# The base product of a feed-forward layer as three rounded products, and later places for GpSimd's weight splits, in an eight-layer fp32 kernel

## The reference

```python
def _L0_ffn_ref(x, W_base, b_base, W_router, A_stack, B_stack):
    logits = xf @ W_router.T
    probs = softmax(logits)
    topk_p, topk_i = top_k(probs, 2); topk_p = topk_p / sum(topk_p)
    combine = sum(one_hot(topk_i, 8) * topk_p[..., None])
    h = einsum('nd,erd->ner', xf, A_stack) * combine[..., None]
    lora_out = einsum('ner,eor->no', h, B_stack) * SCALING
    base_out = xf @ W_base.T + b_base
    return base_out + lora_out
...
# L1 xattn: 16 query heads in 4 groups, head size 96, keys and values from context and latents
# L1 ffn: the same form as L0 ffn.  L2 xattn: one head, Q = x Wq + bq, K = ctx Wk + bk, no values
```

## Time and profile before

| | |
|---|---|
| median of three runs | 1699.91 us |
| profiled execution, its own time | 1700.22 us |
| its span in the trace | 1698.1 us |
| TensorE busy | 1617.2 us, 95% |
| VectorE busy | 931.6 us, 55% |
| ScalarE busy | 743.7 us, 44% |
| GpSimd busy | 371.1 us, 22% |
| L0F from its first base product | 880.15 us |
| L1F from its first base product | 1295.96 us |

### The profile page before, as it was taken

One profiled execution on the slowest core, in us unless ns is written; L12 is line 12 of the kernel. 1 busy time (PEld: TensorE's weight loads), 2 busy tenths in 40 slices (PEclk: granted clock), 3 DMA queues, 4 the chain that ended last, 5 costly groups with the idle time before them and its releaser, 6 DMA issues.

```text
span 1698.1 us, 25834 instructions
## 1 busy us (share of the span) xinstructions
PE 1617.2 (95%) x9028; PEld 1288.3 (76%) x9028; DVE 931.6 (55%) x2467; ACT 743.7 (44%) x2174; POOL 371.1 (22%) x266
## 2 busy tenths in 40 slices
PE   9999999999999999999988999999999899899875
PEld 8888888888888888888764968787876687655454
DVE  5652534525345253452577766757485857455787
ACT  4542443424434244342423453636273231677742
POOL 3210212102121021110014100000002533355452
PEclk9999999999999999999999999999999999999989
DMA  5111101111011010110431000000004212000001
GB/s 183 54 41 49 41 28 52 40 43 47 28 52 41 31 58 28 49 40 27 138 121 65 14 8 6 0 12 0 1 26 158 79 50 90 14 14 14 1 1 49
DMA packets 34137, 76.09 MB, mean 45 GB/s; under 512 B 5536, under 2 KB 18336, under 8 KB 31904
## 3 DMA queue, kind: packets, MB, share of 16 engines
q1 hardware_dynamic: 34080, 75.36, 13.0%
HBM read 73.25 MB, written 2.10 MB: 44 GB/s over the span
## 4 chain that ended last, share of the span: by engine, by line
PE 72%; DVE 17%; ACT 5%; issue 3%; DVEq 2%; POOL 1%; DMA 0%; POOLq 0%; ACTq 0%; SPq 0%
PE banks L973 14%; PE banks L983 10%; PE banks L1070 10%; PE banks L1174 9%; PE banks L1278 5%; PE banks L1250 3%; PE banks L1041 3%; DVE sA L1647 3%; PE banks L1056 2%; ACT sA L673 2%; PE banks L1387 2%; PE banks L1401 2%; PE banks L1380 1%; PE banks L1048 1%; PE banks L1408 1%
## 5 line engine op out<-in xcount | busy, mean ns | idle before, releaser
L1670 DVE TENSOR_TENSOR x_res<-banks,x_res 128x512 f32<-128x512 f32 x120 | 82.9, 692 | 207.6 <-PE banks L1070 207.2
L973 PE MATMUL banks<-cT,w_k 128*128 128x512 f32 x720 | 179.8, 398 | 0.0
L983 PE MATMUL banks<-w_v,cT 128*128 128x512 f32 x768 | 179.8, 392 | 0.0
L973 PE MATMUL banks<-xT,w_q 128*128 128x512 f32 x720 | 175.4, 396 | 0.0
L673 ACT ACTIVATE sA<-sA,nmA 128x128 f32<-128x128 f32 x256 | 99.5, 392 | 166.5 <-DVE nmA L1647 165.5
L1070 PE MATMUL banks<-w_o,atT 128*128 128x512 f32 x720 | 170.3, 393 | 2.1 <-DVE x_res L1670 2.0
L983 PEld LDWEIGHTS banks<-w_v,cT 128*128 128x128 f32 x768 | 142.7, 188 | 28.9
L1070 PEld LDWEIGHTS banks<-w_o,atT 128*128 128x128 f32 x720 | 134.1, 188 | 31.3 <-DVE x_res L1670 2.4
L973 PEld LDWEIGHTS banks<-xT,w_q 128*128 128x128 f32 x720 | 131.9, 188 | 25.5
L973 PEld LDWEIGHTS banks<-cT,w_k 128*128 128x128 f32 x720 | 130.8, 188 | 25.2
L1654 DVE TENSOR_SCALAR rsA<-smA 128x4 f32<-128x4 f32 x64 | 15.7, 245 | 185.5 <-ACT sA L673 185.5
(11 more groups left out here) (243 smaller groups left out, 3257.7 us busy)
## 6 DMA issues: line engine op xcount, KB each, us to landing
w_raw_k<-in_w0k SPq DMA_DIRECT2D x16, 512.0 KB, 3.3
w_raw_v<-in_w0v SPq DMA_DIRECT2D x8, 1024.0 KB, 7.2
w_raw_q<-in_w0q SPq DMA_DIRECT2D x15, 512.0 KB, 3.2
w_raw_o<-in_w0o SPq DMA_DIRECT2D x15, 512.0 KB, 3.2
cTp<-in_ctxT SPq DMA_DIRECT2D x12, 512.0 KB, 4.0
wq_raw<-in_wq SPq DMA_DIRECT2D x1, 3072.0 KB, 11.5
wo<-in_wo SPq DMA_DIRECT2D x1, 3072.0 KB, 21.2
kT<-in_ctxT SPq DMA_DIRECT2D x4, 512.0 KB, 6.5
```

Of the source, the lines that this page charges most:

```text
L973: mm = pe.matmul(dst, w[l][:, c, h * P:(h + 1) * P], t[r][:, c, half * 512:(half + 1) * 512], start=n == 0, stop=n == 3 * DC - 1)
L983: mm = pe.matmul(dst, cT[l][:, c, b * P:(b + 1) * P], wv_[r][:, c, :], start=n == 0, stop=n == 3 * DC - 1)
L1670: dve.tensor_tensor(x_res[:, b, :], bank(6 + b % 2), x_res[:, b, :], ALU.add).then_inc(S("o_added"), 1)
```

## The change

L0F's base product takes the three-product form. Its weight gets a high part `f0p[0]` (ScalarE, in `last_pair` between the second probability store and the second attended store) and a low part `f0p[1]` (GpSimd, behind the split of w_q). TensorE waits for it (`wf_lo`) and, for each block, for xn's low part, which VectorE now makes in L0F too (`PARTS` has L0F). The raw weight and the parts get other places in SBUF, and wq1, wk1 and wv1 are now split in place (the low part is written over the raw weight). The splits of wq1, wq2 and wk2 on GpSimd are cut otherwise and wait for VectorE's xn; wq1's high part is made in four pieces, one for each group of query heads, and TensorE waits for the piece of a group ahead of its queries.

```diff
-PARTS = {L1X: 0, L1F: 1, L2X: 2, L2F: 3}
+PARTS = {L0F: 0, L1X: 1, L1F: 2, L2X: 3, L2F: 4}
...
@@ GpSimd
             split("o", NHP - 1)
             split("q", NHP - 1)
+            pool.wait_ge(S("wf_hi"), 1)
+            for c in range(DC):
+                e = pool.tensor_tensor(f0p[1][:, c, :], ffn["f0"]["base"][:, c, :], f0p[0][:, c, :].bitcast(F32), ALU.subtract)
+            e.then_inc(S("wf_lo"), 1)
...
+            def queries_rest(kv):
+                k = slice(NCH * P * kv, NCH * P * (kv + 1))
+                pool.wait_ge(S("wq1_hi"), kv + 1)
+                pool.tensor_tensor(wq1[1][:, :, k], wq1_raw[:, :, k], wq1[0][:, :, k].bitcast(F32), ALU.subtract)\
+                    .then_inc(S("wq1_lo"), 1)
+
+            def x1_first():
+                pool.wait_ge(S("xn_ready"), NB * (L0F - 1) + NB)
+                queries_rest(0)
+
             def x1_end():
+                pool.wait_ge(S("wkv1_lo"), 2)
+                queries_rest(1)
                 pool.wait_ge(S("ffn_out"), NB)
                 context_rest(0)
-                rest(wq1, wq1_raw, "wq1", 1, 3, DC)
-            pairs_split(pool, ffn_pool(L0F, tb["f0"]), nothing, lambda: rest(wq1, wq1_raw, "wq1", 1, 0, 3), x1_end)
+                queries_rest(2)
+                queries_rest(3)
+            pairs_split(pool, ffn_pool(L0F, tb["f0"]), nothing, x1_first, x1_end)
...
             def x2_end():
+                pool.wait_ge(S("xn_ready"), NB * (L1F - 1) + NB + 2)
+                rest(wk2, raw2["k"], "wk2")
                 context_rest(NPAIR)
-                rest(wk2, raw2["k"], "wk2", 1, 2, DC)

             def x2_weights():
+                pool.wait_ge(S("xn_ready"), NB * (L1F - 1) + NB)
                 rest(wq2, raw2["q"], "wq2")
-                rest(wk2, raw2["k"], "wk2", 1, 0, 2)
...
@@ ScalarE, last_pair
                 store_pT(p, 1)
+                act.wait_ge(S("ffn_ld"), 64)
+                act.activation(f0p[0][:], ffn["f0"]["base"][:], ACT.Copy).then_inc(S("wf_hi"), 1)
                 store_at(p, 1)
...
@@ TensorE, ffn_pe
-                        if second:
-                            wait_parts(L, i, j)
+                        wait_parts(L, i, j)
                         for c in range(DC):
-                            if second:
-                                for n, (l, r) in enumerate(PASSES):
-                                    pe.matmul(bank(4 + j), xnTp[l][:, c, t], f1p[r][:, c, :], start=c == 0 and n == 0, stop=False)
-                            else:
-                                pe.matmul(bank(4 + j), xnT[:, c, t], w["base"][:, c, :], start=c == 0, stop=False)
+                            for n, (l, r) in enumerate(PASSES):
+                                pe.matmul(bank(4 + j), xnTp[l][:, c, t], parts[r][:, c, :], start=c == 0 and n == 0, stop=False)
...
-                if second:
-                    pe.wait_ge(S("wf_lo"), 1)
+                pe.wait_ge(S("wf_lo"), second + 1)
...
@@ TensorE, x1_pe
                     if more:
+                        pe.wait_ge(S("wq1_lo"), kv + 2)
                         queries(kv + 1, 0, 2)
...
@@ VectorE, ahead of L0F's pairs
+            for j in range(2):
+                part_lo(L0F, 0, j)
             ffn_dve(L0F, 4, 2.0)
```

More of the change, by code:

```diff
@@ L133, in build @@
         rr = sb(ctx_a, "rr", [P, NB])
+        f0_high = sb(ctx_a, "f0base_0", [P, DC, D], F32R)
         xw = [xw_all[:, k] for k in range(4)]
@@ L141, in build @@
         ctx_g = ExitStack()
-        ffn["f0"] = dict(base=sb(ctx_g, "f0base", [P, DC, D]), ra=sb(ctx_g, "f0ra", [P, DC, NE + NE * RANK]),
-                         up=sb(ctx_g, "f0up", [P, D]))
+        sb(ctx_g, "f0_pad", [P, 2 * DC * PT2])
+        ffn["f0"] = dict(ra=sb(ctx_g, "f0ra", [P, DC, NE + NE * RANK]), up=sb(ctx_g, "f0up", [P, D]))
         ctx_g.close()
@@ L152, in build @@
         sb(ctx_f, "f0_rest", [P, 32])
+        ctx_g = ExitStack()
+        ffn["f0"]["base"] = sb(ctx_g, "f0base", [P, DC, D])
+        ctx_g.close()
+        ctx_g = ExitStack()
+        f0p = [f0_high, sb(ctx_g, "f0base_1", [P, DC, D], F32R)]
+        ctx_g.close()
         ctx_g = ExitStack()
@@ L210, in build @@
         ctx_x.close()
-        wq1 = [sb(ctx_1, f"wq1_{l}", [P, DC, H1 * HD1], F32R) for l in range(2)]
-        wk1 = [sb(ctx_1, f"wk1_{l}", [P, DC, KV1 * HD1], F32R) for l in range(2)]
-        wv1 = [sb(ctx_1, f"wv1_{l}", [P, DC, KV1 * HD1], F32R) for l in range(2)]
+        in_place, raw1 = {}, {}
+        for n, cols in (("wq1", H1 * HD1), ("wk1", KV1 * HD1), ("wv1", KV1 * HD1)):
+            high_1 = sb(ctx_1, n + "_0", [P, DC, cols], F32R)
+            ctx_x = ExitStack()
+            raw1[n] = sb(ctx_x, n + "_raw", [P, DC, cols])
+            ctx_x.close()
+            in_place[n] = [high_1, sb(ctx_1, n + "_1", [P, DC, cols], F32R)]
+        wq1, wk1, wv1 = (in_place[n] for n in ("wq1", "wk1", "wv1"))
+        wq1_raw, wk1_raw, wv1_raw = (raw1[n] for n in ("wq1", "wk1", "wv1"))
         wo1 = sb(ctx_1, "wo1", [P, NCH * KV1, D])
-        ctx_x = ExitStack()
-        wq1_raw = sb(ctx_x, "wq1_raw", [P, DC, H1 * HD1])
-        ctx_x.close()
         q1 = sb(ctx_1, "q1", [HD1, 2, G1, PT2], F32R)
@@ L534, in _ @@
             pairs_ahead(pool, x1_pool)
-            rest(f1p, ffn["f1"]["base"], "wf")
+            rest(f1p, ffn["f1"]["base"], "wf", 2)
             def x2_end():
+                pool.wait_ge(S("xn_ready"), NB * (L1F - 1) + NB + 2)
+                rest(wk2, raw2["k"], "wk2")
                 context_rest(NPAIR)
-                rest(wk2, raw2["k"], "wk2", 1, 2, DC)
             def x2_weights():
+                pool.wait_ge(S("xn_ready"), NB * (L1F - 1) + NB)
                 rest(wq2, raw2["q"], "wq2")
-                rest(wk2, raw2["k"], "wk2", 1, 0, 2)
             pairs_split(pool, ffn_pool(L1F, tb["f1"]), nothing, x2_weights, x2_end)
@@ L552, in x2_pool @@
                     context_rest(NPAIR + i + 2)
-            pairs_split(pool, x2_pool, lambda: rest(w2, zp2, "wf", 2), nothing, nothing)
+            pairs_split(pool, x2_pool, lambda: rest(w2, zp2, "wf", 3), nothing, nothing)
             rsqrt(NPAIR * (L2F - 1) + 1)
@@ L924, in _, with x1_queries, x1_first @@
             store_xnT(L0F, 0)
-            def x1_queries():
+            def x1_queries(kv):
+                k = slice(NCH * P * kv, NCH * P * (kv + 1))
+                act.activation(wq1[0][:, :, k], wq1_raw[:, :, k], ACT.Copy).then_inc(S("wq1_hi"), 1)
+            def x1_first():
                 act.wait_ge(S("wq1_ld"), 16)
-                high(wq1[0], wq1_raw[:], "wq1")
+                x1_queries(0)
+                x1_queries(1)
             def x1_keys_values():
@@ L932, in x1_keys_values, with x1_end @@
                 high(wv1[0], wv1_raw[:], "wkv1")
-            pairs_split(act, ffn_act(L0F), x1_queries, x1_keys_values, lambda: context_high(0))
+            def x1_end():
+                context_high(0)
+                x1_queries(2)
+                x1_queries(3)
+            pairs_split(act, ffn_act(L0F), x1_first, x1_keys_values, x1_end)
             pairs_ahead(act, x1_act)
@@ L1178, in ffn_pe @@
             def ffn_pe(L, f):
-                w, second = ffn[f], int(L == L1F)
+                w, second, parts = ffn[f], int(L == L1F), f1p if L == L1F else f0p
                 def body(i, last):
@@ L1550, in _ @@
             f3_turn(0)
-            pe.wait_ge(S("wf_lo"), 4)
+            pe.wait_ge(S("wf_lo"), 5)
             f3_gate_up(0)
```

8 lines of the change are left out of this document (2 added, 6 removed).

## The result

| | before | changed |
|---|---|---|
| median of the runs, us | 1700.01 (4 runs) | 1685.66 (4 runs, 1681.33 to 1687.29) |
| ratio | | 0.9913, 95% interval 0.9891 to 0.9934 |
| profiled execution, us | 1700.22 | 1684.36 |
| its span, us | 1698.1 | 1682.0 |
| mean granted clock over the span | 0.984 | 0.986 |

The change makes the kernel 0.9% faster. It is inside what case (a) allowed for itself (1685.5 to 1691.5), but only just.

What follows compares the result with a forecast made beforehand. TensorE bounds the kernel (72% of the chain), stalled in both third pairs by GpSimd's bulk splits holding up VectorE's tiny instructions. 8.7 + 6.7 - 4.2 = 11.2 us gained, giving 1688.7 us; range 1684 to 1693.5.

Steps and rivals of the forecast that it cites:

- case (a): Whole program: both stalls gone, 4 us lost in front, 4 at the two ends; 1688.7 us (1685.5 to 1691.5); chance 0.60.
- L0F, pairs 1 to 3: First feed-forward layer, first three token pairs: 32.8 us where 44.1 stood, 11.3 us won.
- L0F, fourth pair: First feed-forward layer, last pair to the first context product: 17.0 us against 14.37, 2.6 us lost.
- L1F, all: Second feed-forward layer: 8.2 us won in the third pair, 1.5 lost in the fourth, 6.7 us together.
- part 1: Both feed-forward layers: GpSimd's later splits end the third pairs' stalls, so each takes 10.93 us instead of 21.04 and 19.16.
- part 2: First layer's base product in three rounded products: 1.27 us a pair shorter, only 0.60 left because VectorE's cycle bounds it.
- rival (c): New waits at keys and context bring the lower clock and collisions: gain 5 to 8.5 us, 1691.5 to 1695; chance 0.18.
- part 3: Last head pair before the first feed-forward layer: f0base's split delays VectorE 2.9 us, with clock 4.2 lost (0.5 to 6).
- half low-clock stretch: Last head pair: idle growing from 0.9 to 3.9 us brings half a lower-clock stretch, 1.3 us lost.
- (b): Front costs 0.5 us, or periods are 10.17: gain 14.9, with both 17 us, 1683 to 1685.5; chance 0.17.
- (d): Stalls moved into the fourth pairs by splits running into their routing: 7.1 us lost, 1707 us; chance 0.03.
- (e): Whole program: no change that can be told, the gain given back at a transfer; chance 0.02.

Runs made afterwards that it cites:

- E6: The changed kernel run again without a further edit, on one chip with two variants: 1683.29 us, ratio 0.9926 to the kernel before.
- E1: The changed kernel without the rounded product and its f0base split, only the later splits of wq1, wq2 and wk2 kept: 1679.01 us, ratio 0.9899.
- E2: The changed kernel with the splits of wq1, wq2 and wk2 back in their old places, rounded product kept: 1697.29 us, ratio 1.0008.
- E5: The kernel before, with GpSimd's wq1 split in the first layer's third pair cut from three instructions into twelve: 1691.53 us, ratio 0.9978.
- E4: The changed kernel with f0base split earlier, ahead of the w_q split, beside the head pair before: 1683.24 us, ratio 0.9925.
- E8: The changed kernel with GpSimd's f0base split moved behind the last x times gate, second run of this kernel: 1682.05 us, ratio 0.9909.
- E9: The changed kernel with GpSimd's f0base split cut from four instructions into sixteen, same place and bytes: 1682.66 us, ratio 0.9891.
- E3: The changed kernel with GpSimd's f0base split moved behind the last x times gate, first run of this kernel: 1681.07 us, ratio 0.9908.
- E7: The re-timing alone run again, without the rounded product and its f0base split, on another chip: 1681.01 us, ratio 0.9912.

## Why the prediction was right, step by step

| step | forecast | first profile | E6 |
|---|---|---|---|
| L0F, pairs 1 to 3, us | 3 x 10.93 | 10.45, 10.90, 10.80 | 10.46, 10.90, 10.81 |
| L0F, fourth pair | 17.0 | 16.50 | 17.26 |
| L1F, all | 49.3 | 49.78 | 49.77 |
| last head pair of L0X, loss | 4.2 | 2.4 | 2.4 |
| rest of the program, gain | 0 | 2.4 | |

**The stalls (part 1).** Right, in cause and size. E1 has the gain without the product, E2 the stall without the gain, and E5 the mechanism: a tiny VectorE instruction lasts until the GpSimd instruction beside it ends. The sentence that leaned on the Trainium skill, "SBUF — State Buffer", section "Who interferes with whom", stands: an exclusive lock, held for a whole instruction. This trace agrees, with 3304 ns for a one-hot that otherwise takes 279, and 0.88 to 1.04 us beside pieces of 0.99. I had read the one-hots as the place of the stall; two thirds of it were the two instructions on tw in front of them (E5).

**The product's worth (part 2).** Right that the rounded product makes VectorE's cycle the bound: pairs of 10.8 to 10.9, not 10.17. The first pair of L0F is 10.45, 0.5 better than I let it be; after it TensorE's weight load waits 0.3 to 0.5 us for hs in each. In the fourth pair the keys came 11.35 us behind the base product (forecast 11.9) and the wait for the context was 0.58 us (0.7). The forecast of 17.0 lies between the two profiles because of the clock, which I had left to rival (c): in E4, E6, E8 and E9 it is low for 3.4 us in this pair, from 0.1 to 1.6 us behind the start of the keys, which an idle of 2.16 us precedes; in the first profile and in E3 it is not, after the same idle. (A reading of mine was loose: the earlier trace rows has 4.58 us for the 36 key products, and my 4.4 is the distance to the next product. It moves the sum by 0.2 us.)

**L1F.** Forecast 49.3, measured 49.8. What I did not have is the 1.21 us of idle before hs in the fourth pair; without it (E7) the layer takes 48.7, so my sum for the pair was otherwise half a microsecond high. The cause of the idle: wq2's split ends at 1321.6, GpSimd's additions of the bias start only then, one of them blocks ve, and rstd, the one-hots and hs are late. The wait for the context, forecast at 1 to 2 us, is 1.79.

**The last head pair (part 3).** The mechanism was right and its size too large. The delay of the out products is 2.48 us (forecast 2.9); VectorE's and GpSimd's instructions alternate. What failed is the half low-clock stretch, 1.3 us, that I added behind the idle time. The idle was 1.07 us, not 3.9, because TensorE's own products in front were slow: their low clock lay at 860.9 to 867.7, ahead of the wait (869.1 to 870.2), not behind it. E2 shows my case, low clock behind the idle (and over the products in front as well) and 22.73 - 18.78 = 3.95 us lost; so 4.2 was near an upper value and not the middle.

**What the sum did not have.** 9.8 + 6.3 - 2.4 = 13.7 us by the profile, where 8.7 + 6.7 - 4.2 = 11.2 stood. The span became 16.1 us shorter; the other 2.4 us lie behind L1F (from there to the end 346.1 us before, 343.5 in the change; the stretches in front of L0F and between the layers take the small rest), in stages whose work the change leaves as it is. One kernel by itself differs there by more: E1 and E7 are the same and took 338.9 and 343.6 us, with 21.4 and 29.2 us of it at the lower clock. So the 2.4 us need no cause in the change, and none is shown; between the kernel before and the change the time at the lower clock there is equal (35.7 and 36.0 us), so the clock alone does not explain them either. The 3 us between forecast and median are thus in part the over-large price in front and in part this stretch.

**The rivals.** (b) needed a front cost of 0.5 us or periods of 10.17, and neither is there. (c) was half there, in the clock of the fourth pair. (d), the stalls moved into the fourth pair, exists in small: the 1.21 us before hs in L1F. (e) is excluded by the interval.

**Which version.** The prediction had the terms for this and did not add them up: 0.6 us a pair for the product against 4.2 us for its split. The runs show that the product does not pay for its split here: 1.9 to 2.4 us in front (21.18 and 21.22 us against 18.78 in the kernel before and 19.30 and 19.22 in E1 and E7) against 0.3 to 1.1 us in the layer. The re-timing alone (1679.01 and 1681.01 us, ratios 0.9899 and 0.9912) beats the kernel before clearly. That it also beats the changed one by some 2 us is the way the stage profiles point, at the edge of what these runs resolve.

## What to carry to other kernels

Bulk subtractions on GpSimd cost first by where they stand: beside small VectorE instructions on the path three of 3.4 us cost TensorE 7 us of idle, behind the last of them nothing. If they can't move, cut them: the tiny instruction is held for one piece (2.70 us of idle in E5). And a cheaper matmul is worth what the engine that feeds it leaves over: of 1.27 us a pair 0.6 stayed, and the split that it needed had to be hidden somewhere too.
